# Two expert phases of a hybrid layer stack: the shared expert's down products in float32r parts, turned rows kept in DRAM, and one table product on GpSimd

## The chip, the cores and the metric

The kernel is one program on one core of a Trainium2 chip. The metric is the device time of an execution in microseconds, as the median of several runs; the profile shows one execution with every instruction of the engines.

## The reference

Four residual layers over 4096 tokens of width 256, each on a layernorm of its input. The change is in the second and the fourth, which are the same mixture of experts with the same weights:

```python
x = x + _L0_attn_a_ref(_layernorm(x), ...)      # recurrent memory
x = x + _L0_ffn_ref(_layernorm(x), ...)         # experts, phase "moe1"
x = x + _L0_attn_b_ref(_layernorm(x), ...)      # attention
x = x + _L0_ffn_ref(_layernorm(x), ...)         # experts, phase "moe2"

def _L0_ffn_ref(hidden_states, gate_w, w_gate, w_up, w_down, sw_gate, sw_up, sw_down, shared_gate_w):
    E, K, I = (8, 2, 352)
    x = hidden_states.reshape(-1, h)                       # 4096 x 256
    probs = softmax(einsum('th,eh->te', x, gate_w))
    topk_w, topk_i = top_k(probs, K)                       # 2 of 8 experts, weights scaled to sum 1
    eo = einsum('eti,eih->eth', silu(x @ w_gate[e]) * (x @ w_up[e]), w_down)
    out = einsum('te,eth->th', combine, eo)
    sg = sigmoid(x @ shared_gate_w.T)
    so = silu(x @ sw_gate) * (x @ sw_up) @ sw_down         # the shared expert, for every token
    return out + sg * so
```

## The kernel before

Each expert phase (`ffn_phase`) is one sequence of 103 tiles of 128 rows, and every engine walks through it in the same order with one `step(n, kind)` per tile. Tiles 0 to 21 (`NA = 22`) are "shared": the shared expert on 22 of the 32 token tiles. Then come 71 "routed" blocks, in which GpSimd gathers the rows of one expert from DRAM and scatters the results, and 10 "late" tiles, the shared expert on the last ten token tiles. While the shared tiles run, the router works beside them: in tiles 0 to 3 (`LOOK = 4`, the first tiles) each step also normalises seven further token tiles (`extra`, `BESIDE = 7`), stores them to DRAM (`kept`, the tensor `normalised_rows`), transposes them on TensorE, copies them out on ScalarE (`extra_T`) and multiplies them with the router (L803). In tiles 4 to 8 VectorE searches the top two experts and each row's place (`choose_first`, `choose_second`, `counts`, `places`, `positions`, L509 to L603); in tiles 9 to 16 it makes one-hot matrices in eight pieces (`one_hots`, L615, L617, L620) which TensorE multiplies to find the inverse order (`inverse`, L820); then follow the lists of slots (L626 to L639) and the remainders of the routed down weights (L666).

A tile's own work is a chain. TensorE transposes its rows (L786, `rows_in`); ScalarE casts them to float32r (`srcT_high`, L356, `source_out`) and VectorE takes the remainder (L483, `source_rest`). TensorE forms gate and up from three sets of float32r products, high by high, high by the weights' remainder, remainder by high (L865). ScalarE applies SiLU (L372), VectorE multiplies (L674, `hidden`), TensorE transposes the hidden tile (L886, `hidden_T`), ScalarE copies it out (L377, `hidden_out`). In a routed tile the hidden tile is split the same way, with its remainder on VectorE (L658, `hidden_rest`), and the down product is nine float32r products (L909, L907, L909); in a shared or late tile it is three plain float32 products (L914), which the profile shows as six instructions. VectorE then adds the gated result to X (L678, `add_shared`). In the late tiles VectorE also adds the routed results in groups of four tiles (`combine`, L685 and L688, six times).

All orders are written out by hand; the engines meet through semaphores. In step n TensorE does the hidden transposes of tile n-1, gate and up of n, the row transposes of n+1, a table product if one is due, and the down products of n-1; before these it waits until the add of tile n-2 has been done. VectorE in step n does the multiplication of tile n+1, the source remainder of n+2, what belongs to the router, and the add of tile n. Rows of tiles 4 to 21 are loaded from `kept` into `src` by SyncE's queue (L216).

## Time and profile before

| | |
|---|---|
| median of 3 runs | 1951.66 us (1944.48 to 1956.36) |
| the profiled execution | 1932.97 us |
| its span | 1931.2 us |
| TensorE (PE) busy | 1852.4 us (96%) |
| VectorE (DVE) busy | 1353.2 us (70%) |
| ScalarE (ACT) busy | 1172.3 us (61%) |
| GpSimd (POOL) busy | 417.4 us (22%) |
| phase moe1, phase moe2 | about 225 to 634 us, about 1513 to 1931 us |

Busy time of TensorE includes the pipelined ends of its instructions, so what a group of products costs is read from the start of one group to the start of the next. The same holds for VectorE, where the next instruction starts a little before the shown end of the one ahead of it.

### The profile page before, as it was taken

To read this page: it belongs to the slowest core of one execution; us is meant where nothing else is said; L and a number is where in the kernel's file an instruction comes from. 1 tells how busy PE (TensorE), PEld (TensorE's weight loads), DVE (VectorE), ACT (ScalarE), POOL (GpSimd) and SP (SyncE) were. 2 spreads that over 40 slices of the span, in tenths; PEclk is the share of its full clock that TensorE was granted. 3 is DMA by queue.
4 is the path that set the end of the run, shared out by engine and by line. 5 is a ranking of instruction groups with operands and counts; after the bars stand their busy time and mean duration, and the time that the engine had idled before them with its cause. 6 is when DMAs were issued, how large, how long until landed. Compare 5 with 4: busy or idle time off the path is not lost. (4 is left out here: it accounts for less than half of the span.)

```text
span 1931.2 us, 51761 instructions
## 1 busy us (share of the span) xinstructions
PE 1852.4 (96%) x19836; PEld 1432.4 (74%) x19836; DVE 1353.2 (70%) x2724; ACT 1172.3 (61%) x2371; POOL 417.4 (22%) x497
## 2 busy tenths in 40 slices
PE   6899899999999888999999999999998999999998
PEld 4688789999999644555555555565545789999997
DVE  6566678544446777899999999999943878444445
ACT  5221344544445643898999989999895634444443
POOL 1122100455552332000000000000000001555551
PEclk9999999999999999999999999999999999999999
DMA  7000121222226565321221111111004311222228
GB/s 306 1 1 0 53 64 31 69 77 77 79 78 196 144 172 147 79 50 50 49 50 47 41 41 41 41 42 42 3 3 190 107 39 30 78 79 77 74 74 267
DMA packets 86539, 149.13 MB, mean 77 GB/s; under 512 B 35620, under 2 KB 69284, under 8 KB 80612
## 3 DMA queue, kind: packets, MB, share of 16 engines
q1 hardware_dynamic: 68428, 103.24, 17.8%
q0 software_dynamic: 17856, 42.60, 8.0%
q8 instruction: 167, 2.74, 0.6%
q14 instruction: 64, 0.52, 0.1%
q10 hardware_dynamic: 24, 0.02, 0.0%
HBM read 96.68 MB, written 48.76 MB: 75 GB/s over the span
## 5 line engine op out<-in xcount | busy, mean ns | idle before, releaser
L2207 ACT ACTIVATE att_scores_pt<-att_scores_psE 128x512 f32<-128x512 f32 x1024 | 598.4, 598 | 69.0 <-PE att_scores_psE L1711 27.2
L1726 DVE TENSOR_REDUCE att_mx<-att_scores_psS 128x1 f32<-128x1024 f32 x472 | 578.0, 1225 | 50.6 <-PE att_scores_psS L1711 19.4
L1711 PE MATMUL att_scores_psE<-att_qs,att_ks 99*32 99x512 bf16 x4096 | 438.1, 382 | 3.9 <-DVE att_scores_psO L2237 3.2
L2309 PE MATMUL att_scores_psO<-att_scores_pt,att_va 128*17 128x256 f32 x4096 | 330.8, 379 | 2.9 <-ACT att_scores_osb L2212 1.3
L1711 PE MATMUL att_scores_psS<-att_ks,att_qs 96*32 96x512 bf16 x3776 | 308.9, 380 | 0.1
L1711 PEld LDWEIGHTS att_scores_psE<-att_qs,att_ks 99*32 99x32 bf16 x4096 | 136.8, 95 | 103.4 <-ACT att_scores_pt L2207 8.4
L2309 PEld LDWEIGHTS att_scores_psO<-att_scores_pt,att_va 128*17 128x17 f32 x4096 | 132.3, 98 | 102.5 <-issue 13.2
L865 PE MATMUL moe_ps<-W_rest,moe_srcT_high 128*128 (+2 forms) x824 | 200.4, 324 | 0.0
L658 DVE TENSOR_TENSOR moe_hidT_rest<-moe_ps,moe_hidT_high 128x384 fp32r<-128x384 f32 x142 | 79.2, 558 | 156.3 <-ACT moe_hidT_high L377 156.3
L283 POOL DMA_INDIRECT expert_rows<-work,moe_slots_i x142 | 140.3, 988 | 205.4 <-ACT work L399 179.1
L1711 PEld LDWEIGHTS att_scores_psS<-att_ks,att_qs 96*32 96x32 bf16 x3776 | 126.9, 98 | 77.6 <-issue 1.8
L274 POOL DMA_INDIRECT work<-normalised_rows,moe_slots_i x142 | 139.3, 981 | 123.1 <-DVE moe_slots_i L639 79.3
L356 ACT CAST moe_srcT_high<-moe_ps 128x256 fp32r<-128x256 f32 x206 | 76.9, 373 | 144.3 <-PE moe_ps L786 144.2
L865 PE MATMUL moe_ps<-moe_gate_up_high,moe_srcT_high 128*128 x568 | 149.5, 344 | 0.0
L372 ACT ACTIVATE moe_hid<-moe_ps 128x352 f32<-128x352 f32 x206 | 95.6, 464 | 88.0 <-PE moe_ps L865 88.0
L865 PEld LDWEIGHTS moe_ps<-W_rest,moe_srcT_high 128*128 128x128 f32 x824 | 144.9, 189 | 0.1
L865 PE MATMUL moe_ps<-moe_gate_up_high,moe_srcT_rest 128*128 x568 | 138.0, 324 | 0.0
L1734 POOL TENSOR_TENSOR att_mx<-att_mx,att_zeros 128x32 bf16<-128x32 f32 x16 | 4.2, 261 | 618.4 <-DVE att_mx L1726 618.4
L674 DVE TENSOR_TENSOR moe_hid<-moe_hid,moe_ps 128x352 f32<-128x352 f32 x206 | 106.3, 516 | 30.9 <-PE moe_ps L865 30.7
L399 ACT ACTIVATE work<-moe_ps,moe_y_weight 128x256 f32<-128x256 f32 x142 | 67.4, 475 | 96.8 <-PE moe_ps L909 96.8
L653 DVE SCALAR_TENSOR_TENSOR moe_pick<-work,moe_pick 128x2 f32<-128x2 f32 x142 | 22.8, 161 | 114.2 <-PE moe_ps L865 114.2
L786 PE MATMUL moe_ps<-ident,work 128*128 128x128 f32 x524 | 101.6, 277 | 1.2 <-DVE moe_srcT_rest L483 0.5
(327 smaller groups left out, 3224.2 us busy)
## 6 DMA issues: line engine op xcount, KB each, us to landing
W_gate_up<-in_gate_up_dram SPq DMA_DIRECT2D x2, 6346.0 KB, 21.9
work<-expert_rows SPq DMA_DIRECT2D x12, 1024.0 KB, 7.6
query_key_parts<-att_qkv_parts SPq DMA_DIRECT2D x64, 192.0 KB, 3.0
normalised_rows<-work SPq DMA_DIRECT2D x64, 128.0 KB, 1.9
att_qs<-query_key_parts SPq DMA_DIRECT2D x16, 384.0 KB, 4.3
att_ks<-query_key_parts SPq DMA_DIRECT2D x16, 384.0 KB, 4.5
W_down<-in_down_a_dram SPq DMA_DIRECT2D x2, 2304.0 KB, 28.1
work<-normalised_rows SPq DMA_DIRECT2D x36, 128.0 KB, 2.1
```

Of the source, the lines that this page charges most:

```text
L274: nc.gpsimd.indirect_dma_start(out=src[u][:, :], out_offset=None, in_=xn_d, in_offset=bass.IndirectOffsetOnAxis(ap=slots_i[:, j, 0:1].bitc ...
L283: nc.gpsimd.indirect_dma_start(out=ys, out_offset=bass.IndirectOffsetOnAxis(ap=slots_i[:, j, 1:2].bitcast(U32), axis=0), in_=yb[j % 2][:, ...
L356: nc.scalar.copy(srcT_high[u].rearrange("p k t -> p (k t)"), psT[:, 0:D]).then_inc(srcT_ready, 1)
L372: nc.scalar.activation(hid[u][:, 0:I], psG[u][:, 0:I], ACT.Silu).then_inc(silu_done, 1)
L658: nc.vector.tensor_tensor(hidT_rest[:, :, :].rearrange("p k t -> p (k t)"), psH[:, 0:IP], hidT_high[:, :, :].rearrange("p k t -> p (k t)") ...
L674: nc.vector.tensor_tensor(hid[u][:, 0:I], hid[u][:, 0:I], psU[u][:, 0:I], ALU.mult).then_inc(hid_ready, 1)
L786: last = nc.tensor.transpose(bank[:, k * P:(k + 1) * P], u[:, k * P:(k + 1) * P], ident[:, :])
L865: last = nc.tensor.matmul(bank[u][:, 0:width], rows[:, k, :], weights(k), start=(not rows_rest and not weights_rest and k == 0), stop=(row ...
L1711: last = nc.tensor.matmul(out[j:j + 32, :], stationary[:, j:j + 32], moving, start=True, stop=True, tile_position=(0, j), skip_group_check ...
L1726: return nc.vector.tensor_reduce(a.mx[g % 2][:, v:v + 1], bank[:, :, :].rearrange("p h k -> p (h k)"), AX.X, ALU.max)
L2207: nc.scalar.activation(pt[s % 2][:, r, :], psE[use % E_BANKS][:, :], ACT.Exp, scale=HD ** -0.5).then_inc(p_ready, 1)
L2309: last = nc.tensor.matmul(psO[32 * r:32 * r + VC, cols], va[g][:, kt, r * VC:(r + 1) * VC], pt[s % 2][:, r, cols], start=(kt == 0 and part ...
```

## The change

Shared and late tiles now form their down product as routed ones do: the hidden tile is cast to float32r and split, and three sets of three float32r products are made, with a cast copy of the shared down weights (`shared_down_high`) and their remainder in the last part of `down_rest`, both made once a phase at tile 0. Every transposed further tile is stored to DRAM (`turned_rows`) and tiles 4 to 21 load these (18 a phase), so TensorE does not transpose their rows again, and ScalarE casts them straight from the loaded buffer. `extra_T` has seven buffers instead of two, and ScalarE waits for the store of the copy seven tiles ahead. The product of a one-hot piece with the tile numbers is given to GpSimd, with a semaphore `tiles_marked` for which TensorE's table product and VectorE's next piece wait. Some small tensors are moved into `work`.

```diff
         @block.sync
         def _(sp):
+            def store_turned(n):
+                for x in range(n * BESIDE, (n + 1) * BESIDE):
+                    sp.wait_ge(x_srcT, x + 1)
+                    sp.dma_start(xt_d[:, x, :], extra_T[x % BESIDE].rearrange("p k t -> p (k t)")).then_inc(T_stored[x % BESIDE], 16)
+
+            def load_turned(n):
+                x = n - LOOK
+                sp.wait_ge(T_stored[x % BESIDE], 16 * (x // BESIDE + 1))
+                sp.dma_start(src[ring(n)][:, 0:D], xt_d[:, x, :]).then_inc(early_loaded[ring(n) - 2], 16)
+
             for n in range(LOOK):
...
-            for n in range(LOOK, NA):
-                x = n - LOOK
-                sp.wait_ge(x_stored[x % BESIDE], 16 * (x // BESIDE + 1))
-                if n >= LOOK + SRC - 2:
-                    sp.wait_ge(T_done, n - (SRC - 2) + 1)
-                sp.dma_start(src[ring(n)][:, 0:D], kept[:, n, 0:D]).then_inc(early_loaded[ring(n) - 2], 16)
+                if n:
+                    store_turned(n - 1)
+                if n == 2:
+                    for first in range(LOOK, LOOK + SRC - 2):
+                        load_turned(first)
+            store_turned(LOOK - 1)
+            for n in range(LOOK + SRC - 2, NA):
+                sp.wait_ge(srcT_split, n - (SRC - 2) + 1)
+                load_turned(n)
...
             nc.gpsimd.memset(cw[:, :, :], 0.0).then_inc(cw_zero, 1)
+            for i in range(CH // PIECE):
+                pool.wait_ge(hot_ready, i + 1)
+                if i >= 2:
+                    pool.wait_ge(inv_done, i - 1)
+                nc.gpsimd.tensor_tensor(hot_id[i % 2][:, :, 0, :], hot_j[:, :, :],
+                                        tile1[:, i * PIECE:(i + 1) * PIECE, None].to_broadcast([P, PIECE, NBT]), ALU.mult).then_inc(tiles_marked, 1)
...
             def source_out(n, u):
 
-                act.wait_ge(T_done, n + 1)
-                nc.scalar.copy(srcT_high[u].rearrange("p k t -> p (k t)"), psT[:, 0:D]).then_inc(srcT_ready, 1)
+                high = srcT_high[u].rearrange("p k t -> p (k t)")
+                if turned(n):
+                    act.wait_ge(T_done, turns(n))
+                    nc.scalar.copy(high, psT[:, 0:D]).then_inc(srcT_ready, 1)
+                    return
+                act.wait_ge(early_loaded[ring(n) - 2], 16 * ((n - LOOK) // (SRC - 2) + 1))
+                act.wait_ge(u_done, n)
+                nc.scalar.copy(high, buffer(n)[:, 0:D]).then_inc(srcT_ready, 1)
+
+            def shared_down_split_high():
+                nc.scalar.copy(shared_down_high[:, :, :], W["down"][:, :, SHARED, :]).then_inc(shared_down, 1)
...
                         for i in HIGHS[n][BESIDE - 2:]:
                             weights_high(i)
+                    if n == 0:
+                        shared_down_split_high()
                 if n + 1 < NS:
                     source_out(n + 1, (n + 1) % 2)
...
                 nc.vector.tensor_tensor(hot_p[i % 2][:, :, :], iota_p[:, None, :].to_broadcast([P, PIECE, P]),
-                                        over(pos_p, P), ALU.is_equal)
-                dve.wait_ge(hot_ready, i + 1)
-                nc.vector.tensor_tensor(hot_id[i % 2][:, :, 0, :], hot_j[:, :, :], over(tile1, NBT), ALU.mult).then_inc(inv_ready, 1)
+                                        over(pos_p, P), ALU.is_equal).then_inc(inv_ready, 1)
...
-                if k == "routed":
-                    hidden_rest(n)
+                hidden_rest(n)
                 if here + 1 < NS:
                     hidden(n + 1, (here + 1) % 2, buffer(here + 1) if kind(here + 1) == "routed" else None)
                 if k == "shared" and n + 2 < LOOK:
                     extras(n + 2, range(4, BESIDE))
                 if k == "shared" and n < len(RESTS):
                     weights_rest(RESTS[n][1])
+                if n == 0:
+                    dve.wait_ge(shared_down, 1)
+                    nc.vector.tensor_tensor(W["down_rest"][:, :, SHARED, :], W["down"][:, :, SHARED, :], shared_down_high[:, :, :],
+                                            ALU.subtract).then_inc(shared_down_split, 1)
...
-            def down(n, u, e, before, routed=False):
+            def down(n, e, before):
...
+                if n == 0:
+                    pe.wait_ge(shared_down, 1)
+                    pe.wait_ge(shared_down_split, 1)
+                shared = isinstance(e, int) and e == SHARED
+                for stationary, rests in ((hidT_high, False), (hidT_high, True), (hidT_rest, False)):
+                    if stationary is hidT_rest:
+                        pe.wait_ge(hidT_split, n + 1)
+                    for k in (range(KI - 1, -1, -1) if stationary is hidT_rest else range(KI)):
+                        if rests:
+                            weights = W["down_rest"][:, k, e, :]
+                        else:
+                            weights = shared_down_high[:, k, :] if shared else D_high[k][:, e, :]
...
-                rows_in(n + 1, buffer(n + 1), "shared", None)
+                if n + 1 < LOOK:
+                    rows_in(n + 1, buffer(n + 1), "shared", None)
```

How the rows of an engine now stand, at three places. First VectorE in phase moe1, step 0 of the first tiles (`X` is the add of tile 0, `W_rest1_52` the remainders of the gate and up weights). Before:

```order
L479 TENSOR_TENSOR W_rest1_52<-W_gate_up1,moe1_gate_up_high 128x704 x2
L674 TENSOR_TENSOR moe1_hid<-moe1_hid,moe1_ps5 128x352
L487 TENSOR_SCALAR work<-X,mv,rstd 128x256 x3
L479 TENSOR_TENSOR W_rest1_52<-W_gate_up1,moe1_gate_up_high 128x704 x3
L678 SCALAR_TENSOR_TENSOR X<-moe1_ps6,moe1_sg,X 128x256
L483 TENSOR_TENSOR moe1_srcT_rest<-moe1_ps0,moe1_srcT_high 128x256
```

and in the changed kernel:

```order
L516 TENSOR_TENSOR W_rest1_52<-W_gate_up1,moe1_gate_up_high 128x704 x2
L695 TENSOR_TENSOR moe1_hidT_rest_2437<-moe1_ps1,moe1_hidT_high_2436 128x384
L711 TENSOR_TENSOR moe1_hid<-moe1_hid,moe1_ps5 128x352
L524 TENSOR_SCALAR work<-X,mv,rstd 128x256 x3
L516 TENSOR_TENSOR W_rest1_52<-W_gate_up1,moe1_gate_up_high 128x704 x3
L757 TENSOR_TENSOR W_down_rest1_51<-W_down1,moe1_shared_down_high 128x3x256
L715 SCALAR_TENSOR_TENSOR X<-moe1_ps6,moe1_sg,X 128x256
L520 TENSOR_TENSOR moe1_srcT_rest<-moe1_ps0,moe1_srcT_high 128x256
```

The remainder of the hidden tile (L695) stands ahead of the multiplication, and the subtraction for the shared down weights (L757) behind the three weight subtractions and ahead of the add, whose down product on TensorE needs it.

Second VectorE in the step of one one-hot piece. Before:

```order
L674 TENSOR_TENSOR moe1_hid<-moe1_hid,moe1_ps4 128x352
L483 TENSOR_TENSOR moe1_srcT_rest<-moe1_ps0,moe1_srcT_high 128x256
L615 TENSOR_TENSOR work<-moe1_iota_j,moe1_pos_j 128x576
L617 TENSOR_TENSOR work<-moe1_iota_p,moe1_pos_p 128x1024
L620 TENSOR_TENSOR work<-work,moe1_tile1 128x8x72
L678 SCALAR_TENSOR_TENSOR X<-moe1_ps6,moe1_sg,X 128x256
```

and in the changed kernel:

```order
L695 TENSOR_TENSOR moe1_hidT_rest_2437<-moe1_ps1,moe1_hidT_high_2436 128x384
L711 TENSOR_TENSOR moe1_hid<-moe1_hid,moe1_ps4 128x352
L520 TENSOR_TENSOR moe1_srcT_rest<-work,moe1_srcT_high 128x256
L654 TENSOR_TENSOR work<-moe1_iota_j,moe1_pos_j 128x576
L656 TENSOR_TENSOR work<-moe1_iota_p,moe1_pos_p 128x1024
L715 SCALAR_TENSOR_TENSOR X<-moe1_ps6,moe1_sg,X 128x256
```

The product with `tile1` has left the step, and the hidden remainder (L695) has come ahead of the multiplication.

Third TensorE in such a step, from the last gate and up products to the next hidden transposes. Before:

```order
L865 MATMUL moe1_ps5<-moe1_shared_high,moe1_srcT_rest 128x352 x2
L786 MATMUL moe1_ps0<-ident,work 128x128 x2
L820 MATMUL moe1_ps7<-work 128x144 x8
L914 MATMUL moe1_ps6<-W_down1,work 128x256 x3
L886 MATMUL moe1_ps1<-ident,moe1_hid 128x128 x3
```

and in the changed kernel:

```order
L904 MATMUL moe1_ps5<-moe1_shared_high,moe1_srcT_rest 128x352 x2
L861 MATMUL moe1_ps7<-work 128x144 x8
L951 MATMUL moe1_ps6<-moe1_shared_down_high,moe1_hidT_high_2436 128x256 x3
L951 MATMUL moe1_ps6<-W_down_rest1_51,moe1_hidT_high_2436 128x256 x3
L951 MATMUL moe1_ps6<-moe1_shared_down_high,moe1_hidT_rest_2437 128x256 x3
L925 MATMUL moe1_ps1<-ident,moe1_hid 128x128 x3
```

The row transposes (L786) are gone, the table product (L820, now L861) follows the gate and up products at once, and three sets of three float32r products stand in the place of three plain ones.

## Rows read from the trace of the kernel before

**Rows 1.** Groups of instructions, shapes apart: count, busy us, mean ns, idle before

```profile
L658 DVE TENSOR_TENSOR moe_hidT_rest<-moe_ps,moe_hidT_high 128x384 fp32r<-128x384 f32 x142 | 79.2, 558 | 156.3 <-ACT moe_hidT_high L377 156.3
...
L479 DVE TENSOR_TENSOR W_rest<-W_gate_up,moe_gate_up_high 128x704 fp32r<-128x704 f32 x32 | 26.7, 884 | 0.1
...
L620 DVE TENSOR_TENSOR work<-work,moe_tile 128x576 bf16<-128x576 bf16 x16 | 12.0, 752 | 0.0
```

**Rows 2.** TensorE's timeline, moe1: start us, length us, line; a plain shared tile

```profile
331.88 0.38 PE L786 MATMUL moe_ps<-ident,work 128*128 128x128 f32 x2
332.10 1.46 PE L914 MATMUL moe_ps<-W_down,work 128*128 128x256 f32 x6
333.40 0.49 PE L886 MATMUL moe_ps<-ident,moe_hid 128*128 128x128 f32 x3
...
335.68 0.38 PE L786 MATMUL moe_ps<-ident,work 128*128 128x128 f32 x2
```

**Rows 3.** TensorE's timeline around a routed tile's down products

```profile
422.02 0.38 PE L786 MATMUL moe_ps<-ident,work 128*128 128x128 f32 x2
...
423.30 0.49 PE L886 MATMUL moe_ps<-ident,moe_hid 128*128 128x128 f32 x3
```

**Rows 4.** VectorE's timeline, the multiplication of four tiles

```profile
271.69 0.52 DVE L674 TENSOR_TENSOR moe_hid<-moe_hid,moe_ps 128x352 f32<-128x352 f32 x1 [1.33 <-PE moe_ps L865]
...
293.51 0.52 DVE L674 TENSOR_TENSOR moe_hid<-moe_hid,moe_ps 128x352 f32<-128x352 f32 x1 [0.59 <-PE moe_ps L865]
...
327.73 0.52 DVE L674 TENSOR_TENSOR moe_hid<-moe_hid,moe_ps 128x352 f32<-128x352 f32 x1 [0.44 <-PE moe_ps L865]
...
347.92 0.51 DVE L674 TENSOR_TENSOR moe_hid<-moe_hid,moe_ps 128x352 f32<-128x352 f32 x1
```

**Rows 5.** Who waited for whom: VectorE 271.69-293.51, 327.73-347.92, TensorE 226-348: total, times, longest

```profile
DVE moe_hid L674 <- PE moe_ps L865: 2.5, 3, 1.3
...
DVE moe_hid L674 <- PE moe_ps L865: 1.0, 2, 0.6
DVE X L678 <- PE moe_ps L914: 0.9, 2, 0.5
...
PE moe_ps L914 <- DVE X L678: 1.1, 2, 0.8
```

**Rows 6.** Timelines of three engines in the first tiles, moe1

```profile
236.58 0.80 ACT L338 CAST moe_gate_up_high<-W_gate_up 128x704 fp32r<-128x704 f32 x1
237.26 0.39 ACT L356 CAST moe_srcT_high<-moe_ps 128x256 fp32r<-128x256 f32 x1
...
244.37 1.54 PE L914 MATMUL moe_ps<-W_down,work 128*128 128x256 f32 x6
...
247.20 0.61 PE L803 MATMUL moe_ps<-moe_router,work 128*128 128x9 f32 x4 [0.53 <-DVE X L678]
...
244.27 2.49 DVE L479 TENSOR_TENSOR W_rest<-W_gate_up,moe_gate_up_high 128x704 fp32r<-128x704 f32 x3
246.68 0.47 DVE L678 SCALAR_TENSOR_TENSOR X<-moe_ps,moe_sg,X 128x256 f32<-128x256 f32 x1
```

**Rows 7.** VectorE's timeline, late tiles, start and end of the first combine step

```profile
607.47 0.52 DVE L674 TENSOR_TENSOR moe_hid<-moe_hid,moe_ps 128x352 f32<-128x352 f32 x1 [1.80 <-PE moe_ps L865]
...
611.82 0.51 DVE L674 TENSOR_TENSOR moe_hid<-moe_hid,moe_ps 128x352 f32<-128x352 f32 x1
```

**Rows 8.** GpSimd's costliest two-input product, by form

```profile
L1883 POOL TENSOR_TENSOR att_qkv_parts<-att_qkv_rest,att_qkv_parts 128x512 bf16<-128x512 f32 x32 | 36.9, 1164 | 73.4 <-ACT att_qkv_parts L1909 73.4
```

**Rows 9.** Busy us (and count) of each engine by stretch, then granted clock, DMA share, GB/s

```profile
223.00:226.00 3.00, 1.18 (x3) 0.30 (x2) 1.18 (x6) 0.45 (x3) 0.73 (x5) 1.00 0.01 3
226.00:229.00 3.00, 2.63 (x7) 1.06 (x7) 2.92 (x7) 2.01 (x5) 1.04 (x6) 0.71 0.38 131
229.00:232.00 3.00, 2.90 (x16) 2.56 (x14) 2.95 (x18) 2.10 (x4) 0.00 (x0) 0.72 0.18 64
...
634.00:640.00 6.00, 2.90 (x13) 1.33 (x11) 2.78 (x16) 1.56 (x4) 0.13 (x1) 1.00 0.14 26
```

86 lines of the change are left out of this document (40 added, 46 removed).

## The prediction, made before the changed kernel ran

> **What bounds the kernel now.** I read the times of SiLU (ScalarE, one per tile) first: the two expert phases hold 206 tiles, and outside them nothing changes. The 142 routed ones are untouched. The 64 shared tiles are where the change acts. In a plain one TensorE does 0.22 us of row transposes, 1.30 us of down products and 2.28 us of hidden transposes, gate and up (each from one start to the next), 3.80 in all, with no gap [rows 2]. That is not so everywhere. In the first tiles TensorE waits twice for the residual add on VectorE (0.53 us in the row shown), and during the search for the top two experts it waits 1.1 us in two waits for the same add [rows 5, 6]. There VectorE is the one that sets the step. So the question is less what TensorE saves than what VectorE, which gets a new instruction in all 64 tiles, can afford.
>
> **TensorE's savings.** Three plain float32 products (six instructions) become nine float32r ones. In a routed tile transposes and nine products take 423.30 - 422.02 = 1.28 us, in a shared one 333.40 - 331.88 = 1.52 [rows 2, 3]: 0.24 us less per tile, 32 tiles a phase. The rows of tiles 4 to 21 come turned from DRAM, so 0.22 us of transposes go 18 times a phase [rows 2]. If all of it showed, a phase would give 7.7 + 4.0 = 11.7 us and the program 23.
>
> **VectorE's additions.** The remainder of the hidden tile is now taken in every tile: 558 ns, and since consecutive instructions overlap by 0.08 us (three of 884 ns take 2.49), 0.48 us of its time [rows 1, 6]. In the eight one-hot steps the product with the tile numbers leaves: 752 ns, 0.67 net [rows 1]. So VectorE gains 0.19 us in eight steps and loses 0.48 in 24, in each phase. Where it is the bound, that decides.
>
> **Search steps (VectorE's steps 4 to 8).** From 271.69 to 293.51 us there are five, 21.82 us, in which VectorE waits 1.15 us for TensorE (2.5 in three waits, less the 1.33 that lies ahead of the first row) [rows 4, 5]. It works 20.67; with five remainders 23.1, against 3.80 - 0.24 - 0.22 = 3.34 us of TensorE a step. So these get longer, by 1.25 us, and what TensorE saves buys nothing here.
>
> **One-hot steps (eight, 293.51 to 327.73, 34.22 us).** The mean is 4.28 a step, and TensorE, with a table product in each but the first, is full; VectorE waits 0.44 in such a step and works about 3.9 [rows 4]. TensorE falls by 0.24 + 0.22 to about 3.9, VectorE by 0.19 to 3.7. So TensorE stays the bound in seven of the eight, 0.46 each; in the first VectorE is, 0.19 gained. -3.4 us.
>
> **Five steps to the first routed tiles (327.73 to 347.92, 20.19 us).** VectorE carries the slot lists and twelve down-weight remainders. It waited 1.0 + 0.9 us for TensorE, 0.44 of it ahead of the stretch [rows 4, 5], and so worked 18.7; four hidden remainders are added (the fifth stands there already): 20.6, more than TensorE's 17.9 with what it saves. +0.4. By these three stretches a phase gains 1.75 us where TensorE alone would give 8.
>
> **The first tiles.** ScalarE gets a cast of 128x768 ahead of the cast that lets tile 1 start. The next instruction starts 0.68 us after a cast of 704 columns does, with no gap [rows 6], so 768 take 0.75: +0.75 at tile 1. VectorE gets the remainder (0.48) and then the 128x768 subtraction (0.87, from 884 ns for 704 columns [rows 1]), *behind* the three gate/up subtractions that end at 246.68, and TensorE's down products of tile 0, which began at 244.37, now wait for it [rows 6]. They start at 246.68 + 0.75 + 0.48 + 0.87 = 248.8, the add can begin 1.06 + 0.2 later, at 250.05, where it began at 246.68. So the next tile is 3.4 us late, not 2.1, and TensorE stands 3.7 us. One more remainder lies on the chain in the following step (TensorE waits for the add already): +0.48. From tile 2 on TensorE leads: -0.24 at tile 3, and at tile 4 -0.24 and -0.22. Together +3.85 - 0.7 = +3.15.
>
> **The late ten.** Tiles outside the combine save 0.24 and their transposes stay: three steps and the two last down products, -1.2. In the six combine steps VectorE stands only some 0.2 of the 3.80 us and goes to about 4.08. The step that opens them took 4.35 (607.47 to 611.82) and takes 4.60, the next five lose 0.28 each [rows 7]. Together +1.65 - 1.2, +0.3 with the lag that cannot be recovered.
>
> **Edits at nothing.** 56 stores of turned rows and 36 loads from another tensor: SyncE's queue is idle most of a step, and the store that ScalarE's copy 7 tiles later waits for lands about 0.5 us after that copy was due, under the waits named above. GpSimd's product is 576 columns; its product of 512 took 1164 ns [rows 8], so about 1.3 us, with some 1.8 us before TensorE's table product wants it. Between the 0.75 that VectorE needed and that 1.8 nobody waits; at 2.5 us each of sixteen would cost 0.7.
>
> **Sum.** Per phase -1.75 + 3.15 + 0.3 = +1.7, 3.4 for both. A wait of 3.7 us on TensorE can also cost clock. At 223 to 226 it was busy 1.18 of 3 us and the granted clock then was 0.71; at 634 to 640 it was busy 2.90 of 6 us and kept 1.00 [rows 9]. The clock of 0.71 and 0.72 in two stretches of 3 us is 3.4 us at 1.2 GHz and the rest at 2.4 [rows 9], so one such drop costs up to 1.7 us of work. I take half of that in each phase: +1.7. The profiled execution took 1932.97 us (span 1931.2) and would take 1938; the median of the runs shown lies 1.0% above it, and the same 5 us give **1957**.
>
> The Trainium skill (TensorE: Matmul & The Clock Gate, Part 1) says that the throttled state is the default and activity releases it. By that every longer wait is at risk, though the 634 to 640 row shows one that kept its clock.
>
> **Rivals.**
> 1. *The remainder hides.* By the table of the profile TensorE is busy 96% of the span and VectorE 70%, and in routed tiles the same instruction lies under TensorE's work. Then both phases keep their savings less the first tile's cost: -23 + 2 x 4 = -15, 1937. Against it: the steps above have VectorE without a gap. 8 in 100.
> 2. *It costs clock in the search* (the other side). With 3.34 us of work in steps of 3.9 to 5.3 TensorE is busy under 70%, where it was busy 94% at clock 1.00. If the granted clock falls to 1.2 GHz in that stretch, 3.34 becomes 6.7 and passes VectorE by 1.5 to 2 us a step: five steps, two phases, +15 to 20 on the sum, 1972 to 1977. It decides once the clock falls in over half of these steps. The 634 to 640 row speaks against. 11 in 100.
> 3. *GpSimd is slow beside VectorE.* It runs while VectorE makes the 128x1024 one-hot, from two inputs in SBUF. Beyond 1.8 us TensorE waits at each table product; at 2.5 us 16 x 0.7 = +11, 1968. No row shows a GpSimd product beside such an instruction. 8 in 100. The Trainium skill (GPSIMD Engine Reference, section 1) names just this: its SBUF interface is shared with VectorE, with contention when VectorE has two SBUF inputs; it gives no price.
> 4. *Nothing of it matters*, both signs cancel within 2 us: 1952. 10 in 100.
>
> The forecast itself has 63 in 100, with 1949 to 1964 as its own range (from no clock loss and hidden late remainders to two drops a phase).
>
> **Range and chances.** A measurement of this kernel tells about 1% (20 us) from no change. Rival 2 whole, and a little of rival 3, lie above 1971; under 1932 lies only a fraction of rival 1. Faster 0.04, same 0.84, slower 0.12. From 1940 to 1972 leaves out part of rival 1 and most of rival 2.
>
> **What would show it.** Right: down products of shared tiles at 1.06 us; steps of 3.9 us with table products, 3.55 in plain late tiles, 4.08 in the combine; search steps of 3.9 to 5.3 us in which TensorE waits over 1 us for the residual add; a wait of over 3 us ahead of the first down product. Wrong: no such waits, or search steps shorter than before; GpSimd's product over 1.8 us and waited for; a granted clock under 1 within the search.

## The result: 13 us slower where 5 were forecast

| | before | after |
|---|---|---|
| median | 1950.92 us (1944.48 to 1956.36, 6 runs) | 1964.82 us (1956.15 to 1967.32, 6 runs) |
| the profiled execution, its span | 1932.97, 1931.2 us | 1956.15, 1954.4 us |
| mean granted TensorE clock | 0.991 | 0.984 |

The ratio is 1.0066, with a 95% interval of 1.0039 to 1.0093: slower, by less than the 1% that a measurement of this kernel tells from no change, and inside the forecast range of 1940 to 1972. The loss is 13 us by the ratio (the medians themselves lie 13.9 us apart) and 23 by the two profiled executions. Both numbers need an explanation, and they turn out to have different ones.

**Where the time went.** Read ScalarE's SiLU again, one row per tile. These are tiles 0 to 4 of moe1 in the changed kernel (start us, length us, engine and line, and in brackets the idle time ahead and who ended it):

```profile
231.07 0.47 ACT L408 ACTIVATE moe_hid<-moe_ps 128x352 f32<-128x352 f32 x1
...
240.03 0.50 ACT L408 ACTIVATE moe_hid<-moe_ps 128x352 f32<-128x352 f32 x1
...
254.61 0.46 ACT L408 ACTIVATE moe_hid<-moe_ps 128x352 f32<-128x352 f32 x1 [0.84 <-PE moe_ps L904]
...
264.51 0.46 ACT L408 ACTIVATE moe_hid<-moe_ps 128x352 f32<-128x352 f32 x1 [0.63 <-PE moe_ps L904]
...
272.45 0.46 ACT L408 ACTIVATE moe_hid<-moe_ps 128x352 f32<-128x352 f32 x1 [1.45 <-PE moe_ps L904]
```

In the kernel before, the same five stand at 231.76, 239.70, 249.13, 258.55 and 266.72. The steps were 7.94, 9.43, 9.42 and 8.17 and are 8.96, 14.58, 9.90 and 7.94. In moe2 they were 9.06, 9.43, 9.42, 8.17 and are 9.59, 16.76, 9.95, 7.93. One step, from tile 1 to tile 2, holds nearly all of it. Going on by the same rows through both phases:

| SiLU of tile | before, moe1 / moe2 | after, moe1 / moe2 | difference |
|---|---|---|---|
| 0 to 4, first tiles | 34.96 / 36.08 | 41.38 / 44.23 | +6.4 / +8.2 |
| 4 to 23, search, one-hots, slot lists | 79.67 / 79.64 | 77.91 / 77.91 | -1.8 / -1.7 |
| 23 to 93, routed tiles | 248.95 / 248.97 | 253.47 / 254.83 | +4.5 / +5.9 |
| 93 to 102, late tiles | 33.95 / 34.17 | 34.77 / 34.76 | +0.8 / +0.6 |

The third line is odd: the change touches nothing in the routed tiles. The experiments come back to it.

**The first down products.** TensorE's timeline in step 1 of moe1, with the wait that the prediction spoke of, and VectorE's at the same place:

```profile
244.09 0.61 PE L843 MATMUL moe_ps<-moe_router,work 128*128 128x9 f32 x4
248.44 0.98 PE L951 MATMUL moe_ps<-moe_shared_down_high,moe_hidT_high 128*128 128x256 f32 x3 [3.73 <-DVE W_down_rest L757]
249.21 0.84 PE L951 MATMUL moe_ps<-W_down_rest,moe_hidT_high 128*128 128x256 f32 x3
249.85 0.84 PE L951 MATMUL moe_ps<-moe_shared_down_high,moe_hidT_rest 128*128 128x256 f32 x3
250.49 1.05 PE L826 MATMUL moe_ps<-ident,work 128*128 128x128 f32 x4
```

```profile
244.93 2.48 DVE L516 TENSOR_TENSOR W_rest<-W_gate_up,moe_gate_up_high 128x704 fp32r<-128x704 f32 x3
247.34 0.95 DVE L757 TENSOR_TENSOR W_down_rest<-W_down,moe_shared_down_high 128x768 fp32r<-128x768 f32 x1
250.73 0.48 DVE L715 SCALAR_TENSOR_TENSOR X<-moe_ps,moe_sg,X 128x256 f32<-128x256 f32 x1 [2.44 <-PE moe_ps L951]
```

The subtraction of the shared down weights (L757) lies behind the three gate/up ones (L516), and the down products of tile 0 wait 3.73 us for it; 3.7 was forecast. They start at 248.44 (248.8 forecast; tile 0 came 0.69 us earlier here, so against it they are 0.3 us later than forecast). But then nine products take 250.49 - 248.44 = 2.05 us where 1.06 stood in the sum. The windows say why (us; busy us and count of PE, PEld, DVE, ACT, POOL; granted clock; DMA share; GB/s):

```profile
243.00:246.00 3.00, 1.64 (x13) 1.23 (x11) 3.00 (x8) 2.67 (x6) 0.00 (x0) 1.00 0.49 166
246.00:249.00 3.00, 0.56 (x3) 0.59 (x3) 2.29 (x3) 0.00 (x0) 0.00 (x0) 0.65 0.78 265
249.00:252.00 3.00, 3.00 (x16) 3.00 (x16) 0.92 (x3) 0.74 (x2) 0.00 (x0) 0.50 0.79 227
252.00:255.00 3.00, 3.00 (x19) 3.00 (x19) 1.19 (x4) 1.24 (x4) 0.00 (x0) 0.71 0.41 135
```

Here, in moe1, the granted clock falls at 246.9, within the wait (244.7 to 248.4), and the work behind the wait runs at 0.50, which is 1.2 GHz. In moe2 it is at 0.50 already from 1537.1 on, 10 us ahead of the long wait (3.21 us, from 1547.6 to 1550.8), here with TensorE busy all the time:

```profile
1538.00:1541.00 3.00, 3.00 (x16) 3.00 (x14) 0.51 (x2) 1.10 (x5) 0.00 (x0) 0.50 0.66 223
```

**The later stretches** are near the forecast. VectorE's multiplications of the same four tiles as in [rows 4]:

```profile
276.96 0.52 DVE L711 TENSOR_TENSOR moe_hid<-moe_hid,moe_ps 128x352 f32<-128x352 f32 x1 [0.64 <-PE moe_ps L904]
...
299.71 0.51 DVE L711 TENSOR_TENSOR moe_hid<-moe_hid,moe_ps 128x352 f32<-128x352 f32 x1
...
331.58 0.52 DVE L711 TENSOR_TENSOR moe_hid<-moe_hid,moe_ps 128x352 f32<-128x352 f32 x1 [0.32 <-PE moe_ps L904]
...
351.90 0.51 DVE L711 TENSOR_TENSOR moe_hid<-moe_hid,moe_ps 128x352 f32<-128x352 f32 x1
```

Search 22.75 us (21.82 before), one-hots 31.87 (34.22), slot lists 20.32 (20.19). TensorE in a plain shared tile, beside [rows 2]:

```profile
335.45 0.51 PE L951 MATMUL moe_ps<-moe_shared_down_high,moe_hidT_high 128*128 128x256 f32 x3
335.80 0.52 PE L951 MATMUL moe_ps<-W_down_rest,moe_hidT_high 128*128 128x256 f32 x3
336.16 0.52 PE L951 MATMUL moe_ps<-moe_shared_down_high,moe_hidT_rest 128*128 128x256 f32 x3
336.52 0.49 PE L925 MATMUL moe_ps<-ident,moe_hid 128*128 128x128 f32 x3
```

Nine products in 1.07 us and no row transposes. And the opening of the combine and its next step, beside [rows 7]:

```profile
615.49 0.52 DVE L711 TENSOR_TENSOR moe_hid<-moe_hid,moe_ps 128x352 f32<-128x352 f32 x1 [0.89 <-PE moe_ps L904]
...
620.08 0.51 DVE L711 TENSOR_TENSOR moe_hid<-moe_hid,moe_ps 128x352 f32<-128x352 f32 x1
...
624.17 0.51 DVE L711 TENSOR_TENSOR moe_hid<-moe_hid,moe_ps 128x352 f32<-128x352 f32 x1
```

4.59 and 4.09 us. GpSimd's new product, and three rows of TensorE's waits of moe1, 226 to 352 us (in all, times, longest):

```profile
L288 POOL TENSOR_TENSOR work<-work,moe_tile 128x576 bf16<-128x576 bf16 x16 | 32.0, 2003 | 27.4 <-DVE work L654 27.4
```

```profile
PE moe_ps L951 <- DVE W_down_rest L757: 3.7, 1, 3.7
PE moe_ps L951 <- DVE X L715: 3.2, 5, 1.5
...
PE moe_ps L861 <- POOL work L288: 0.4, 1, 0.4
```

The product takes 2.00 us on the mean, not 1.3, but TensorE waited for it only once in this phase, for 0.4 us. It is the add on VectorE (L715) that TensorE waits for instead.

### The profile page after: what moved, and what is told of

Read it like the earlier page. It is cut to its first block and busy times, and to the rows that moved or that the text cites. A ratio compares the mean times of both kernels' runs of the same rounds, so it can differ in the third digit from the quotient of the medians.

```text
span 1954.4 us, 52187 instructions
## 1 busy us (share of the span) xinstructions
PE 1847.6 (95%) x19956; PEld 1429.2 (73%) x19956; DVE 1374.0 (70%) x2774; ACT 1185.6 (61%) x2373; POOL 448.2 (23%) x513
## 5 line engine op out<-in xcount | busy, mean ns | idle before, releaser
L695 DVE TENSOR_TENSOR moe_hidT_rest<-moe_ps,moe_hidT_high 128x384 fp32r<-128x384 f32 x206 | 114.2, 554 | 192.1 <-ACT moe_hidT_high L412 182.6
L412 ACT CAST moe_hidT_high<-moe_ps 128x384 fp32r<-128x384 f32 x206 | 98.5, 478 | 86.2 <-PE moe_ps L925 74.3
L385 ACT CAST moe_srcT_high<-moe_ps 128x256 fp32r<-128x256 f32 x170 | 63.3, 372 | 131.4 <-PE moe_ps L826 115.6
L925 PE MATMUL moe_ps<-ident,moe_hid 128*128 128x128 f32 x618 | 102.6, 275 | 6.0 <-DVE moe_hid L711 3.6
```

Of the source, the lines that this page charges most:

```text
L412: nc.scalar.copy(hidT_high[:, :, :].rearrange("p k t -> p (k t)"), psH[:, 0:IP]).then_inc(hidT_ready, 1)
L695: nc.vector.tensor_tensor(hidT_rest[:, :, :].rearrange("p k t -> p (k t)"), psH[:, 0:IP], hidT_high[:, :, :].rearrange("p k t -> p (k t)") ...
L925: last = nc.tensor.transpose(psH[:, k * P:(k + 1) * P], hid[u][:, k * P:(k + 1) * P], ident[:, :])
```

## The experiments

Twelve runs, two of them repeats, were made in three groups, each with its own runs of the kernel before (medians 1937.5, 1944.5 and 1945.7 us), so only the ratios compare between groups. "First tiles" is SiLU of tile 0 to tile 4, moe1 / moe2.

| kernel | ratio to before, 95% | first tiles, us |
|---|---|---|
| before, profiled twice | 1 | 34.96 / 36.08 and 34.98 / 36.07 |
| after | 1.0066 [1.0039, 1.0093] | 41.4 / 44.2 |
| after_again | 1.0061 [1.0043, 1.0078] | 44.8 / 45.1 |
| kept_running | 1.0021 [1.0006, 1.0036] | 39.0 / 40.2 |
| down_first | 1.0042 [1.0023, 1.0060] | 42.4 / 43.3 |
| first_plain | 1.0004 [0.9986, 1.0023] | 40.4 / 36.8 |
| until_one_hots | 0.9998 [0.9983, 1.0013] | 37.5 / 36.1 |
| vector_product | 1.0060 [1.0039, 1.0081] | 44.8 / 41.0 |
| downs_alone | 1.0084 [1.0059, 1.0109] | 45.4 / 44.8 |
| no_split_downs | 0.9986 [0.9970, 1.0003] | 40.3 / 40.0 |
| turned_kept_running | 0.9972 [0.9957, 0.9987] | 35.6 / 36.5 |
| stores_between | 0.9955 [0.9936, 0.9973] | 37.9 / 36.1 |
| stores_between_running | 0.9960 [0.9942, 0.9979] | 35.4 / 35.4 |

### The same two kernels once more

> The changed kernel once more, unaltered. In its first profile the 70 steps of the routed tiles (SiLU of tile 23 to that of tile 93) took 253.5 and 254.8 us, where they took 249.0 in the kernel before, in both phases, with steps of 6.2 and 7.6 us at tile 79 in which ScalarE and VectorE stood for a reason that the trace calls remote; four kernels that share its routed tiles took 249.0 to 249.2. If this belongs to the program: 253 to 255 again, and about 10 us of the difference of the two profiled executions is a cost of the change that no term of the prediction has. If it belongs to that execution: 249 us, and the ratio to before stays at 1.004 to 1.009 from the first tiles (6 to 8 us a phase), the later shared tiles (-1.8) and the late ones (+0.8).

> The kernel before once more, unaltered, so the ratio is 1. Its first profile shows 9.43 us from SiLU of tile 1 to that of tile 2 in both phases, where three kernels with plain down products in these tiles took 12.9 to 13.7 us in at least one phase, at a granted clock of 0.5 for more than ten us. If that fall of the clock comes with what the change does there (its store waits, the later casts): 9.4 us again, and n0 to n4 at 35 to 36. If the kernel before has it too in some executions: 13 us in one or both phases, and its span in that profile is about 4 us longer for each.

Measured: the changed kernel gave 1.0061, with 253.95 and 252.28 us in the routed tiles. The kernel before gave 1.0004 with 253.88 and 255.30 us there, where its first profile has 249.0. So the extra 3 to 6 us a phase in the routed tiles do not belong to the change. They go with the group of runs: all eight phases profiled in the first group (first_plain, down_first, kept_running, no_split_downs) took 248.9 to 249.2 us, and all sixteen of the other two groups 250.2 to 255.3. ScalarE's rows at tile 79 in the second profile of the kernel before, where the step is 6.80 us:

```profile
549.80 0.48 ACT L378 CAST moe_hidT_high<-moe_ps 128x384 fp32r<-128x384 f32 x1 [0.28 <-PE moe_ps L887]
553.37 0.46 ACT L373 ACTIVATE moe_hid<-moe_ps 128x352 f32<-128x352 f32 x1 [3.08 <-remote]
```

ScalarE stands for 3.08 us, released by nothing that an engine of this core did. The same stands in moe2 of the changed kernel (2.40 us at 1859.91). Of the 23 us between the first two profiles 10.4 are this; the rest, 12.5, agrees with the 13 by the ratio. In the first tiles the kernel before repeated its steps to 0.02 us, with 9.42 and 9.43 us from tile 1 to 2. The changed kernel gave 17.26 and 17.28 there, after 14.58 and 16.76: that step is long in all four phases, by a varying amount.

### Is the loss in the first tiles, and is it the wait or the clock?

Tiles 0 to 2 with plain products; cast and subtraction in step 3:

```diff
+        PLAIN = set(range(3))
...
-                if n == 0:
+                if n == 3:
                     dve.wait_ge(shared_down, 1)
...
+                if n in PLAIN:
+                    for k in range(KI):
+                        last = nc.tensor.matmul(psD[:, 0:D], part(k * P, P), W["down"][:, k, e, :],
+                                                start=(k == 0), stop=(k == KI - 1))
+                    last.then_inc(d_done, 1)
+                    return
```

> The changed kernel, but tiles 0 to 2 of each phase keep the plain float32 down products, and the cast and the subtraction of the shared expert's down weights stand in step 3 of ScalarE and VectorE. Theory (the first tiles are the term that I sized too small, 6.4 and 8.2 us where 3.15 stood): from SiLU of tile 0 to that of tile 4 it takes 34.3 to 35 us in both phases, as in the kernel before less 0.2 to 0.7, against 41.4 and 44.2 in the changed one. With what the later stretches measured in the changed kernel (-1.3 and +0.7) a phase then costs about -1, and the time is that of the kernel before less 0 to 3 us (ratio 0.9985 to 1.000). Rival (the loss lies in what the tiles 4 on keep, and the first tiles only show it): the ratio stays above 1.004.

Measured 1.0004 [0.9986, 1.0023]: without the split in tiles 0 to 2 the loss is gone as far as the interval (-3 to +4.5 us) can tell, and the rival (above 1.004) is out. The edit takes the wait, three hidden remainders and, by moving it to step 3, the cast out of these tiles together, so it gives the place and not yet the cause. In moe2 the first tiles took 36.81. In moe1 they took 40.40; I had expected 34.3 to 35 in both, and there is more on that below.

One instruction moved, the subtraction ahead of three others on VectorE:

```diff
                     extras(n + 2, range(4, BESIDE))
-                if k == "shared" and n < len(RESTS):
-                    weights_rest(RESTS[n][1])
                 if n == 0:
                     dve.wait_ge(shared_down, 1)
...
+                if k == "shared" and n < len(RESTS):
+                    weights_rest(RESTS[n][1])
```

> The changed kernel, with one instruction of VectorE moved: the subtraction of the shared expert's down weights stands ahead of the three gate/up subtractions of step 0 and not behind them. By the rows of the changed kernel these three take 2.48 us and TensorE's wait is 3.73, so it falls to about 1.25, and the add of tile 0 begins behind the three, at 248.4 where it began at 250.73: -2.3 us a phase if only the wait counts. If the granted clock stays at 1.00 because of the shorter wait, 1 us for the down products and 1.6 for the 3.3 us behind them at 1.2 GHz come back as well: -4 to -5 a phase. The two give 4.6 and about 9 us under the changed kernel (ratio to before 1.004 and 1.002). Rival (the queue of the add behind the subtractions is what counts, wherever the wait lies): less than 1 us a phase.

Measured 1.0042, the higher of the two ratios expected. Of the long wait 0.81 us are left, but the clock had fallen long before it: at 239.6, as the wait of 1.06 us that ends at 240.60 began. TensorE's rows and two of the windows (columns as above):

```profile
240.60 0.66 PE L826 MATMUL moe_ps<-ident,work 128*128 128x128 f32 x2 [1.06 <-DVE moe_srcT_rest L520]
...
252.16 0.98 PE L951 MATMUL moe_ps<-moe_shared_down_high,moe_hidT_high 128*128 128x256 f32 x3 [0.81 <-DVE W_down_rest L755]
```

```profile
238.00:242.00 4.00, 2.78 (x18) 2.51 (x17) 1.54 (x5) 2.47 (x7) 0.00 (x0) 0.70 0.55 188
...
246.00:250.00 4.00, 4.00 (x21) 4.00 (x20) 3.19 (x6) 2.00 (x5) 0.00 (x0) 0.50 0.18 64
```

TensorE then worked for more than ten us at 0.50, so that a wait of 0.81 was left for the down products and the step took 14.87 us. By the ratios (1.0061 to 1.0042) the move gave back 3.7 of 12 us, but the two intervals overlap, and the first tiles took 42.4 and 43.3 us where the changed kernel has 41.4 to 45.1: that it gained anything is not shown. The lost clock was still paid.

The wait left as it is, and products of ones on TensorE in it:

```diff
                 if n == 0:
+                    pe.wait_ge(sg_done, 1)
+                    keep_running(nc, psG[0], ones, 4)
                     pe.wait_ge(shared_down, 1)
...
+                if n == 1:
+                    keep_running(nc, psG[1], ones, 1)
                 extra_in(first + 1)
```

> The changed kernel with TensorE kept busy in its two long waits of step 1: one product of ones (512 columns, plain float32, about 0.86 us) ahead of the transposes that waited 1.05 us, and four (3.4 us) ahead of the down products of tile 0, which waited 3.2 to 3.7 us. Their results are never read. The wait itself stays; only the clock can come back. If the loss beyond the forecast is clock: the down products of tile 0 take 1.06 us in place of 2.05, and the first tiles 38.5 to 39 us in both phases (41.4 and 44.2 in the changed kernel), -2.6 and -5.4, 8 us in all. If it is more wait than I worked out and the clock is not what costs: 41 to 45 us as now, or longer by what the products of ones add.

Measured 1.0021, 8 us under the changed kernel, and 39.03 and 40.23 us in the first tiles. TensorE's rows around the down products, and the windows:

```profile
247.30 3.68 PE L53 MATMUL moe_ps<-ones 128*128 128x512 f32 x8
251.18 0.59 PE L953 MATMUL moe_ps<-moe_shared_down_high,moe_hidT_high 128*128 128x256 f32 x3 [0.20 <-DVE W_down_rest L757]
```

```profile
246.00:249.00 3.00, 2.93 (x15) 1.84 (x15) 3.00 (x7) 2.42 (x5) 0.00 (x0) 1.00 0.46 155
249.00:252.00 3.00, 2.80 (x12) 1.42 (x11) 2.03 (x3) 0.00 (x0) 0.00 (x0) 1.00 0.77 264
252.00:255.00 3.00, 2.96 (x26) 2.85 (x24) 2.03 (x6) 1.41 (x4) 0.00 (x0) 1.00 0.80 232
```

The down products still wait for the same subtraction, until 251.18, but the clock is 1.00 from 228 to 264 us, and in moe2 from 1517 to 1559. So the loss splits: 4.1 us a phase over the kernel before (39.0 against 35.0, 40.2 against 36.1) are wait and longer steps, for which the forecast had 3.15. What the changed kernel has above that, 2.4 to 5.8 us a phase over two profiles of it, is clock, for which it had 0.85. The edit fills two waits, that of 1.06 us with one product and the long one with four, so it does not say at which of them the clock is lost. The windows of the changed kernel's second profile do (moe1, columns as above):

```profile
234.00:238.00 4.00, 3.77 (x30) 3.24 (x29) 1.75 (x4) 3.83 (x8) 0.00 (x0) 0.91 0.61 203
238.00:242.00 4.00, 3.75 (x17) 3.69 (x16) 1.54 (x5) 1.92 (x6) 0.00 (x0) 0.50 0.78 267
...
250.00:254.00 4.00, 0.78 (x4) 0.76 (x4) 3.13 (x4) 0.49 (x1) 0.00 (x0) 0.50 0.65 223
```

A mean of 0.91 over the first row, with the clock at 1.00 and then at 0.50, puts the fall at 237.2, ahead of both waits: the longest wait of TensorE in the nine us before is 0.25 us, the one for the source remainder has shrunk to 0.25 (at 239.31), and the long one comes only at 250.05. Five profiles have the wait for the subtraction and no added products of ones (two of the changed kernel, down_first, vector_product and downs_alone). In two of their ten phases the clock fell within this wait and stayed at 0.50 for 6.8 us; in the other eight it fell 10 to 13 us ahead of it and stayed there for 17 to 20.5 us. So the longer and dearer falls do not come from the long wait.

### Each part by itself

Plain products in all shared tiles, so turned rows and GpSimd's product alone:

```diff
+        PLAIN = set([*range(NA), *range(LAST, NS)])
...
-                    if n == 0:
-                        shared_down_split_high()
-                hidden_rest(n)
+                if n not in PLAIN:
+                    hidden_rest(n)
```

> The changed kernel with plain float32 down products in all shared tiles, so without the cast, the subtraction and the 64 remainders: turned rows and GpSimd's product alone. By the terms of the prediction: 0.22 us in tiles 4 and on where TensorE is the bound, that is eight one-hot steps (-1.8) and five behind them (-1.0), nothing in the search, nothing in the late tiles: about -3 us a phase, 6 under the kernel before (ratio 0.997), the first tiles as before. So the split of the downs would be what costs, 19 us of the 13 net. If turned rows show in the search too (18 x 0.22): -4 a phase, 0.996. Rival (turned rows cost by SyncE's queue or by the wait of ScalarE's copy for a store, 1.43 us in one row): ratio 1.000 or above, with n0 to n4 longer than 35 us.

Measured 0.9986, not told from no change. Both halves of the expectation came partly true. From tile 4 to 23 a phase takes 77.76 and 77.62 us against 79.67 and 79.64, -2 where I had -3; of it at most 0.3 lies in the search, by VectorE's multiplications (21.66 and 21.54 us against 21.82). But the first tiles took 40.3 and 40.0.

The split and GpSimd's product alone; tiles 4 to 21 load their rows unturned:

```diff
-        turned = lambda n: not LOOK <= n < NA
-        turns = lambda n: n + 1 if n < LOOK else n + 1 - (NA - LOOK)
+        turned = lambda n: True
+        turns = lambda n: n + 1
...
-                if n:
-                    store_turned(n - 1)
```

> The changed kernel without the turned rows: tiles 4 to 21 load their rows as in the kernel before and TensorE turns them, and no turned row is stored. The split of the down products and GpSimd's product stay. If the first tiles lose by the split alone: the wait of TensorE for the subtraction is 3.2 to 3.7 us, with a clock of 0.5 behind it, and n0 to n4 is 41 to 45 us as in the changed kernel; the search is longer than in the kernel before by 0.7 us (by VectorE) or shorter; ratio 1.006 to 1.009. If the fall of the clock belongs to the turned rows: n0 to n4 38.5 to 39 us (the wait alone), ratio 1.003 to 1.005.

Measured 1.0084, the slowest of all, with 45.4 and 44.8 us in the first tiles and a wait of 3.21 us for the subtraction in each phase (to 255.10 and 1556.81). The clock fell at 240.3 and at 1540.8, 12 and 13 us ahead of these waits, and stayed at 0.50 for 20.5 us. So this fall needs neither the turned rows nor the long wait ahead of it. In the search VectorE's multiplications of tiles 5 and 10 lie 22.63 and 22.92 us apart (21.82 before, 21.66 and 21.54 without the split): the remainders cost 0.8 to 1.1 us there, and the turned rows buy 0.2.

The product of the one-hots back on VectorE:

```diff
-                nc.gpsimd.tensor_tensor(hot_id[i % 2][:, :, 0, :], hot_j[:, :, :],
-                                        tile1[:, i * PIECE:(i + 1) * PIECE, None].to_broadcast([P, PIECE, NBT]), ALU.mult).then_inc(tiles_marked, 1)
...
+                dve.wait_ge(hot_ready, i + 1)
+                nc.vector.tensor_tensor(hot_id[i % 2][:, :, 0, :], hot_j[:, :, :], over(tile1, NBT), ALU.mult).then_inc(inv_ready, 1)
```

> The changed kernel with the product of the one-hot and the tile numbers back on VectorE (752 ns in the kernel before), and nothing for GpSimd there. In the changed kernel GpSimd's product took 2.06 us beside VectorE's one-hot of 1.2, over the 1.8 us that were worked out as free. By VectorE's load: its steps with a table product, 3.7 us of work and now 4.4, get to 4.4 us against TensorE's 3.9: 9 to 18 takes 37.5 + 8 x 0.5 = 41 us, +4 a phase, ratio 1.0066 + 0.004 = 1.011. Rival (GpSimd's 2.06 us already sets these steps, so that the move gained little): 37.5 to 39 us, ratio 1.007 to 1.008.

Measured 1.0060 against 1.0061: no difference that can be told. By the profile the eight one-hot steps take 32.93 us in both phases, where the changed kernel has 31.9 and 32.2 (both its profiles): the move is worth about 1 us a phase. I had expected 4, by adding 0.67 us to a VectorE load of 3.7. The steps took 4.12 us (32.93 over eight) with the product in them, so the load without it is 3.45 at most and was put too high.

The split only where TensorE is the bound, from the one-hot steps on:

```diff
+        PLAIN = set(range(9))
...
-                if n == 0:
+                if n == 9:
                     dve.wait_ge(shared_down, 1)
```

> The changed kernel with plain float32 down products in tiles 0 to 8 (no remainder of the hidden tile there), the cast of the shared expert's down weights at the end of step 8 and their subtraction in step 9, so the split only from the one-hot steps on, where TensorE is the bound. By the step of the prediction that says VectorE sets the search: tiles 4 to 9 take 20.4 us as without any split (22.6 to 22.9 where the split begins at tile 3), 9 to 18 37.5 to 38.0, 18 to 23 19.3 to 19.7, the late ones 34.8. Sum with the first tiles as before: 2 us a phase under the kernel before, less 0.6 of the late ones: ratio 0.998 to 0.999. If instead the split pays everywhere but in the first tile, it is no better than the kernel with the split from tile 3 (1.0004).

Measured 0.9998, above the 0.998 to 0.999 expected. The search was as foreseen (20.39 and 20.42 us from SiLU of tile 4 to 9). But the one-hot steps took 32.94 and 33.23 us by VectorE's multiplications, and 33.04 without any split: the split, with its one subtraction, gains nothing even there, and the late tiles still lose 0.8. The changed kernel does have shorter one-hot steps, 31.87 us, but pays for them in its search (22.75 against 21.66): from tile 4 to 23 it takes 77.91 us, the kernel without any split 77.76 and 77.62. The split saves TensorE 0.24 us a tile, and no kernel here shows a place where that is left at the end.

### What lets the clock fall where TensorE hardly waits

The expected gain of the turned rows was going into a step of 12.9 to 13.7 us from tile 1 to tile 2. Compare two profiles with the same waits of TensorE up to 238.6 us. The kernel before, second profile:

```profile
234.00:238.00 4.00, 3.77 (x34) 3.24 (x32) 1.82 (x5) 3.84 (x9) 0.00 (x0) 1.00 0.60 201
238.00:242.00 4.00, 3.67 (x30) 3.61 (x29) 2.70 (x8) 2.95 (x10) 0.00 (x0) 1.00 0.50 174
242.00:246.00 4.00, 3.93 (x29) 3.42 (x28) 4.00 (x8) 3.54 (x7) 0.00 (x0) 1.00 0.39 137
```

And first_plain:

```profile
234.00:238.00 4.00, 3.77 (x33) 3.25 (x32) 1.76 (x4) 3.83 (x8) 0.00 (x0) 1.00 0.53 178
238.00:242.00 4.00, 3.67 (x17) 3.45 (x17) 1.54 (x5) 1.54 (x7) 0.00 (x0) 0.57 0.78 267
242.00:246.00 4.00, 4.00 (x20) 4.00 (x18) 2.86 (x5) 2.10 (x4) 0.00 (x0) 0.50 0.63 218
```

Up to 238 us TensorE is busy for the same 3.77 of 4 us, and its waits are 0.16 and then 0.33 us in both. Yet the clock stays at 1.00 in the one and falls at 238.5 in the other: the 3.67 busy us of its second row hold 17 instructions and not 30. What does differ is around it: the order of the transfers (from 236 to 238.5 the DMA share is 0.49 and 0.79) and ScalarE, whose copy waits for the store of a turned row. In no_split_downs that is 2.08 us:

```profile
241.43 0.37 ACT L372 COPY work<-moe_ps 128x256 f32<-128x256 f32 x1 [2.08 <-DMA turned_rows<-work]
```

Two edits on no_split_downs, alone and together. One product of ones ahead of the transposes that wait 0.33 us:

```diff
+                if n == 1:
+                    keep_running(nc, psG[1], ones, 1)
                 extra_in(first + 1)
```

> The changed kernel with plain down products in all shared tiles (turned rows and GpSimd's product alone), and one product of ones (0.86 us) on TensorE in step 1, ahead of the transposes after which the clock fell in the same kernel without it. There SiLU of tile 1 to that of tile 2 took 13.7 and 12.9 us at a granted clock of 0.50, and 9.43 in the kernel before. If TensorE's short idle time (0.16 and 0.33 us in a row) decides it: 9.4 to 9.9 us now in both phases, and the gain of the turned rows is left: about 3 us a phase from tile 4 on, ratio 0.994 to 0.996. If the fall comes from elsewhere (the same idle times stand in the kernel before, where the clock stays at 1.00): 12 to 14 us again, ratio 0.998 to 1.000.

And the stores of turned rows one by one between SyncE's other stores:

```diff
                     sp.dma_start(kept[:, LOOK + x, 0:D], extra_src[x % BESIDE]).then_inc(x_stored[x % BESIDE], 16)
-                if n:
-                    store_turned(n - 1)
+                    if n:
+                        store_turned(x - BESIDE)
```

> The changed kernel with plain down products in all shared tiles, and the stores of the turned rows issued one by one between SyncE's other stores, and not in a row of seven behind them. The copy of ScalarE that waited 1.4 to 2.3 us for the first of these stores (at 239 to 241 us) should then not wait over 0.3 us. If this wait is what puts step 1 out of its pace and lets the clock fall: SiLU of tile 1 to tile 2 9.4 to 9.9 us, ratio 0.994 to 0.996. If the wait lies under other work, as my prediction had it: no change against the same kernel without the move (0.9986), 12.9 to 13.7 us at a clock of 0.5 in at least one phase.

> Both edits together on the changed kernel with plain down products in all shared tiles: the stores of the turned rows between the others, and one product of ones on TensorE in step 1. If either cures the fall of the clock, this does: n0 to n4 at 34.5 to 36.5 us in both phases, ratio 0.994 to 0.996, the fastest of all. If it is still 39 to 40 us, the fall has another cause and the turned rows gain nothing that can be measured (0.998 to 1.000).

Measured: 0.9972 with the product of ones (0.994 to 0.996 expected), and 9.30 and 9.28 us from tile 1 to 2. 0.9955 with the stores moved, and 11.31 and 9.42 (9.4 to 9.9 expected in both). 0.9960 with both, and 9.42 in both phases. With the stores moved ScalarE's copy no longer waits (the cast of tile 1's rows and then the copy, without a gap):

```profile
238.84 0.39 ACT L388 CAST moe_srcT_high<-moe_ps 128x256 fp32r<-128x256 f32 x1
239.18 0.37 ACT L372 COPY work<-moe_ps 128x256 f32<-128x256 f32 x1
```

The clock fell in moe1 all the same, for 6.8 us. So the wait of that copy is not what decides. It is not free either: in moe2 TensorE waited for the late copy, 1.03 us in no_split_downs and 0.82 in turned_kept_running, and the step from tile 0 to 1 took 9.42 and 9.64 us there, 9.08 and 8.38 in the two kernels with the stores moved. Over all kernels with turned rows and no long wait the step was over 10 us in 5 of 8 phases without the product of ones and in 0 of 4 with it, and in 0 of 4 of the kernel before. (The kernel before has a fall too, in moe2 at 1524.3 us, 5 us behind SiLU of tile 0 like some of the long ones; it lasts 3.4 us.) With both edits, the two windows that were at 0.57 and 0.50 in first_plain:

```profile
238.00:242.00 4.00, 4.00 (x28) 3.47 (x28) 2.36 (x8) 2.52 (x9) 0.00 (x0) 1.00 0.78 265
242.00:246.00 4.00, 3.93 (x30) 3.51 (x29) 4.00 (x8) 3.80 (x8) 0.00 (x0) 1.00 0.74 251
```

The three intervals overlap, so which of the edits is worth more stays open; that the turned rows with either are 5 to 9 us faster than the kernel before (0.9972 to 0.9955) is measured, all three intervals lying under 1. That is the version to keep: turned rows, GpSimd's product, plain float32 down products.

## Why the prediction came out as it did

The sign and the place were right and the size was not: 5 us were forecast and 13 measured, in the range but above the forecast's own 1949 to 1964 by 1 us. Term by term, a phase:

- **The three stretches behind the first tiles**, -1.75: measured -1.29 and -1.28 by the rows that the terms were made from. The search was +0.93 and +1.00 for +1.25, the one-hots -2.35 and -2.08 for -3.4, the slot lists +0.13 and -0.20 for +0.4. The claim that what TensorE saves buys nothing in the search held in both single-part kernels.
- **The one-hot steps** are the term of these that was too large. Steps of 3.9 us were forecast and alternate between 3.9 and 4.1. GpSimd's product took 2.0 us and not 1.3, but TensorE's waits for it sum to 1.1 us in the whole program, so rival 3 (+11 us) did not come. The Trainium skill (GPSIMD Engine Reference, section 1) names contention with VectorE and gives no price; here the shortest product took 1.59 us, and the median 2.06, beside VectorE's one-hots of 1.22.
- **The late ten**: the opening step 4.59 for 4.60, the combine steps 4.09 to 4.11 for 4.08. SiLU shows +0.8 and +0.6, without the two last down products (-0.5 in my sum), so +0.3 fits, but my own terms, 1.65 - 1.2, made 0.45, and the step from there to 0.3 had no row behind it.
- **The first tiles**, +3.15, with half a drop of the clock, +0.85: this is the term that was sized wrong. The wait was 3.73 us for 3.7. With the clock held the same kernel costs +4.1, 0.9 more than forecast: up to tile 2 it lost 3.81 us in moe1 where 3.37 stood, and in the two steps from tile 2 to 4 it lost 0.25 (+0.48 and -0.23) where my terms add up to 0.48 - 0.24 - 0.46 = -0.22. The larger miss is the clock. I sized a fall by two stretches of 0.71, as 1.7 us at most, gave it a half and tied it to the wait of 3.7 us. Measured it is 2.4 to 5.8 us a phase, in every phase. It fell within that wait only in the mildest of them (moe1 of the first profile, at 0.50 from 246.9 to 253.7); in the other three it fell 10 to 13 us earlier and stayed at 0.50 for 17 to 20.5 us, through the whole of step 1, which is packed with TensorE's small products. That the time still lies in the range is owed to the room that it gave to two drops a phase and to the rivals.
- **Stores and loads at nothing**: wrong. The copy of ScalarE waited 1.43 us for a store in the row of the changed kernel and 2.08 to 2.34 in two others, since seven stores stand behind seven others in SyncE's queue. In some phases that cost nothing; in others TensorE waited for the late copy, 0.71 us in moe1 of until_one_hots and 1.03 in moe2 of no_split_downs.
- **Rival 2** (clock falls in the search) did not come: the granted clock was 1.00 from 268 to 346 us. That a fall of the clock costs time was right, its place was wrong. The search has TensorE busy 82% (18.74 of 22.75 us), where I had put it under 70, although my own five steps of 23.1 us in all make it 72. A low busy share is also not what the rows show ahead of a fall: the clock held at 82% there and fell behind 3.77 of 4 busy us in the second profile's step 0.
- **Rival 1** (the remainder hides) is out: the search is longer by 0.93 and 1.00 us (1.25 forecast) and the combine steps by 0.29 to 0.31 (0.28 forecast).

The Trainium skill (TensorE: Matmul & The Clock Gate, Part 1) says that activity releases the throttle. The products of ones agree: each kernel with them kept 1.00 through step 1. What the rule does not tell is the pair of profiles above, the same activity up to 238 us and 1.00 in one and 0.57 in the other behind it.

What stays open: why the clock falls around step 1 and then stays down, in kernels with the turned rows alone, with the split alone and with both, and not in the kernel before. Busy DMA engines alone don't do it (0.78 at a clock of 1.00 in the last rows shown), nor does the wait of ScalarE's copy, nor the long wait of TensorE. What is left, ScalarE's pace, the order of the transfers or chance by execution, was not told apart, and 4 and 8 phases are few.

## What to carry to other kernels

Price a change in a packed stretch of TensorE by the clock that it can cost and not only by the wait that it adds: beside 4.1 us of wait and longer steps a phase lost 2.4 to 5.8 us because its products ran at half the clock. And look up when the clock fell before a wait is named as its cause: in eight of ten phases it fell 10 to 13 us ahead of the longest one. Before a split into float32r parts, find the engine that makes the remainder; a saving of 0.24 us on TensorE for 0.48 on VectorE pays only where VectorE has that much over in the same step, and here it paid nowhere. And when a store is added to a queue, ask what waits for its completion and what stands ahead of it.

## What the runs showed that was not expected

- A product of ones of 0.86 us in a gap of a third of a microsecond went with a clock of 1.00 through step 1 in four of four phases. The same work without it was over 10 us in that step in five of eight.
- The clock can fall with TensorE busy 3.77 of 4 us and no wait over 0.25 us in the nine us before (second profile of the changed kernel, 237.2 us), and stay at half for 20.5 us.
- An execution can carry 1 to 6 us a phase in the routed tiles that no instruction of the core explains. It came at tile 79 to 81 in the kernel before as in the changed one: 249.0 us in one profile and 253.9 and 255.3 in the next, and it was in every profile of the second and third group of runs and in none of the first. A single pair of profiles (23 us here) can double a difference that the ratio puts at 13.
- GpSimd's product of 128x576 took 1.59 us once and 2.06 on the median beside VectorE's wide one-hots.
